# Cross-attention keys made in the opening of the self-attention in front, norm and queries batch by batch in its loop, masks by quarters

## The reference

```python
# both, per head: softmax(q @ k.T * 8**-0.5 + mask) @ v, then a projection
L0_attn  (sublayer 0):  q, k, v from norm(x); no mask
L0_xattn (sublayer 1):  q from norm(x); k, v from ctx; mask: valid keys of each batch (a row per batch)
L3_attn  (sublayer 9):  q, k, v by a down projection to 32 and up again; full 256 x 256 mask
L3_xattn (sublayer 10): q from norm(x); k, v from ctx; full 256 x 512 mask
```

## Time and profile before

| | us |
|---|---|
| median of 3 runs | 1529.12 (1528.99 to 1529.28) |
| the profiled execution | 1515.46 |
| its span, first to last instruction | 1513.4 |
| mean granted TensorE clock | 0.882 |
| PE / DVE / ACT / POOL busy | 1214.5 / 915.8 / 695.4 / 252.3 |

### The profile page before, as it was taken

How to read it: one execution, slowest core, us unless ns; L and a number is a source line. 1 busy time by engine, 2 the same in 40 slices (tenths; PEclk the granted TensorE clock), 3 DMA queues, 4 the chain that set the end, 5 groups by cost and what they waited for, 6 DMA issues and landing times. The chain is left out here.

```text
span 1513.4 us, 25902 instructions
## 1 busy us (share of the span) xinstructions
PE 1214.5 (80%) x9175; PEld 746.5 (49%) x9217; DVE 915.8 (61%) x2378; ACT 695.4 (46%) x1316; POOL 252.3 (17%) x525
## 2 busy tenths in 40 slices
PE   3877997686596398567999999999949669869993
PEld 1333434584243398355666666666638524323332
DVE  5658874334576454775676766666641365487746
ACT  2654883132442022213666665656605225436653
POOL 1211210453010255100000000000017312121110
PEclk8797999898798599677999999999968869979995
DMA  5525111584702466100000000000047451051100
GB/s 148 128 84 142 54 30 79 187 280 133 155 2 91 145 233 214 27 1 0 1 1 1 1 2 1 1 1 1 1 127 230 124 136 24 2 139 44 41 3 14
DMA packets 85600, 114.55 MB, mean 76 GB/s; under 512 B 11281, under 2 KB 65758, under 8 KB 85198
## 3 DMA queue, kind: packets, MB, share of 16 engines
q1 hardware_dynamic: 81026, 103.78, 23.2%
q0 software_dynamic: 4448, 9.12, 2.1%
HBM read 85.79 MB, written 26.61 MB: 74 GB/s over the span
## 5 line engine op out<-in xcount | busy, mean ns | idle before, releaser
L664 DVE TENSOR_REDUCE mx<-ps 128x4 f32<-128x1024 f32 (+1 forms) x128 | 153.4, 1221 | 53.2 <-PE ps L601 44.8
L2240 DVE CUSTOM_DVE_ANT_0 wring<-ps,probs 128x768 f32<-128x768 f32 x128 | 122.5, 957 | 57.0 <-PE ps L2112 56.8
L807 PE MATMUL ps<-probs,vaug 128*32 128x256 f32 (+1 forms) x1792 | 143.4, 394 | 13.4 <-ACT probs L775 9.2
L2196 ACT COPY qs<-ps 128x768 f32<-128x768 f32 x128 | 102.3, 800 | 97.7 <-PE ps L2119 97.7
L765 ACT ACTIVATE probs<-ps 128x1024 f32<-128x1024 f32 x96 | 98.2, 1023 | 86.5 <-PE ps L639 86.5
L770 ACT ACTIVATE probs<-ps 128x512 f32<-128x512 f32 x192 | 106.2, 594 | 38.7 <-PE ps L727 36.7
L236 POOL TENSOR_TENSOR rstd<-veps,mhalf 128x8 f32<-128x8 f32 x14 | 23.2, 1657 | 595.2 <-DVE veps L221 564.9
L2178 ACT ACTIVATE wring<-wring,r 128x768 f32<-128x768 f32 x128 | 120.8, 944 | 2.9 <-DVE r L2243 2.9
L2119 PE MATMUL ps<-ident,wring 128*128 128x128 f32 x768 | 110.4, 281 | 3.2 <-DVE wring L2277 3.2
L601 PE MATMUL ps<-ks,qs 49*128 49x256 bf16 (+1 forms) x512 | 84.0, 369 | 27.2 <-DVE mx L659 10.6
L2119 PEld LDWEIGHTS ps<-ident,wring 128*128 128x128 f32 x768 | 84.6, 141 | 39.4 <-issue 35.3
(11 more groups left out here) (311 smaller groups left out, 2334.2 us busy)
## 6 DMA issues: line engine op xcount, KB each, us to landing
wring<-in_L_ffn_w SPq DMA_DIRECT2D x19, 768.0 KB, 5.8
wring<-in_L_ffn_w SPq DMA_DIRECT2D x32, 384.0 KB, 4.6
wring<-in_L_ffn_w SPq DMA_DIRECT2D x19, 514.0 KB, 4.9
scr_q<-probs SPq DMA_DIRECT2D x10, 384.0 KB, 3.5
scr_k<-probs SPq DMA_DIRECT2D x27, 128.0 KB, 4.1
qs<-scr_q SPq DMA_DIRECT2D x18, 192.0 KB
probs<-in_L_ffn_w SPq DMA_DIRECT2D x8, 384.0 KB, 4.5
probs<-in_L_ffn_w SPq DMA_DIRECT2D x4, 768.0 KB, 6.3
```

The lines of the kernel that those rows point to most:

```text
L664: dve.tensor_reduce(out, src, AX.X, ALU.max, negate=True).then_inc(a_max.sem, 1)
L807: ins = pe.matmul(ps[32 * j:32 * j + 32, self.av_bank(s), q0:S], vaug[:, s % 2, kt, j, :], probs[:, s % 2, j, at:at + S - q0], start=(kt = ...
L2196: act.copy(self.pT[:, g % 2, j, :, k * P:(k + 1) * P], self.buffer("turn", i, 0, KV).rearrange("p (t n) -> p t n", n=P)).then_inc(self.out ...
L2240: dve.tensor_tensor_reduce(self.sc[:, s, :], src, self.maskb[:, u // (2 * PR), :], 1.0, -3.0e38, ALU.add, ALU.max, self.top[:, s:s + 1]).t ...
```

## The change

Two pairs are linked, L0_attn to L0_xattn and L3_attn to L3_xattn (`next`, `prev`).

- Keys of the cross-attention: all four projections in the opening of the self-attention, behind its values (`keys_tensor`); ScalarE evicts and casts part one (`keys_scalar`). In the first groups of its loop GpSimd subtracts (`key_r_gpsimd`), ScalarE casts part two behind the turned maxima (`key_p2_scalar`), GpSimd writes part three (`key_p3_gpsimd`). `ahead_sync` spills them between groups 4 and 9.
- Norm and queries: as a batch of the self-attention is summed, its statistics, power, `h`, transposes and query projection run in the loop of the next batch (`ahead_at`, `ahead_masked_at` say at which step; `beside` for TensorE, `evicted` for ScalarE). Batch 3 has only its statistics there; the rest is in the loop of the cross-attention, which also makes the values.
- SyncE loads keys and queries of batch 0 in groups 11 and 15; for that it waits at group 10 until the self-attention has read the part of `ks` that they overwrite. Mask rows of L0_xattn are written per batch, and cast on GpSimd in the opening. `ctxT`, the early weights and `mask_row` are loaded at the very start, so `late_inputs` has bundles for eleven groups, not thirteen.
- `x_done` is kept between the two; norm, projections and the idle matmuls of the cross-attention are gone.
- A mask pair is four matmuls of 64x64 (`mask_tensor`): row half `r` of the array makes bank `at + r`, in two column halves; the crosswise halves come from copies of the masks with their partition halves swapped (`m3a_half`, `m3x_half`, four DMAs before sublayer 9).

The core of the diff:

```diff
+        def keys_tensor(self, pe):
+            if self.n == 1:
+                pe.wait_ge(written, 16 * 4)
+            pe.wait_ge(proj_f.sem, proj_f.at(self.n - 1, 4))
+            for i in range(B):
+                pe.matmul(bank(i), wt(f"{self.name}_k"), ctxT[:, i * S2:(i + 1) * S2], start=True, stop=True).then_inc(proj_mm.sem, 1)
...
+        def keys_scalar(self, act):
...
+                act.activation(self.key_full(i), bank(i), ACT.Identity, bias=bcol[:, col:col + 1]).then_inc(proj_f.sem, 1)
...
+                act.copy(self.key_part(i, 0), self.key_full(i)).then_inc(proj_p1.sem, 1)
+        def key_r_gpsimd(self, pool, i):
...
+            pool.tensor_tensor(self.key_full(i), self.key_full(i), self.key_part(i, 0), ALU.subtract).then_inc(proj_r.sem, 1)
...
+        def stats_vector(self, dve, b):
+            dve.wait_ge(y_out.sem, y_out.at(self.n - 1, b + 1))
+            for j in (2 * b, 2 * b + 1):
+                ins = dve.bn_stats(stats[:, j, :], x[:, j, :])
...
+        def hT_tensor(self, pe, b):
+            pe.wait_ge(ln_h.sem, ln_h.at(self.norm, b + 1))
...
+            for t in range(2):
+                ins = pe.transpose(bank(6, S + t * P, S + t * P + P), h[:, 2 * b + t, :], ident[:, :])
...
+        def q_scalar(self, act, b):
...
+            act.activation(self.q_full(b), bank(6, S, 2 * S), ACT.Identity, bias=bscaled[:, col:col + 1], scale=SCALE).then_inc(proj_f.sem, 1)
+            act.wait_ge(proj_f.sem, proj_f.at(n, 4 + b + 1))
+            act.copy(self.q_part(b, 0), self.q_full(b)).then_inc(proj_p1.sem, 1)
...
+        def ahead_sync(self, sp, g):
+            n = self.n
+            if 4 <= g < 10:
+                for j in (2 * g - 8, 2 * g - 7):
+                    self.key_spill_sync(sp, j % 4, j // 4)
+            if g == 10:
+                sp.wait_ge(b_mm.sem, b_mm.at(n - 1, 2 * NQ * units[n - 1]))
+                if self.mask == "row":
+                    self.mask_sync(sp, 0)
+            if g == 11:
+                self.key_load_sync(sp, 0, 0, 8)
+            if 12 <= g < 15:
+                self.q_spill_sync(sp, 0, g - 12)
+            if g == 15:
+                self.q_load_sync(sp, 0, 0, 8)
+        def late_sync(self, sp):
+            for b in (1, 2):
+                for k in range(3):
+                    self.q_spill_sync(sp, b, k)
+            sp.wait_ge(b_mm.sem, b_mm.at(self.n - 1, G * units[self.n - 1]))
+        def ahead_at(self, s, u):
+            if self.next:
+                steps = {(9, 2): "n_stats", (10, 0): "n_h", (12, 0): "qr", (12, 2): "qp2", (13, 0): "qp3"}
+                for b in range(B):
+                    what = steps.get((s - 4 * b, u))
+                    if what and (b < 3 or what == "n_stats"):
+                        yield what, b, 0
+            elif self.prev:
+                steps = {(0, 2): [("val", 0), ("val", 1)], (0, 3): [("n_h", 3)], (0, 4): [("v_sb", 1)], (0, 6): [("v_sb", 0), ("val", 2), ("val", 3)],
+                         (1, 0): [("v_sb", 2)], (1, 2): [("v_sb", 3)], (6, 2): [("qr", 3)],
+                         (6, 5): [("qp2", 3)], (7, 2): [("qp3", 3)]}
...
+        def ahead_masked_at(self, t):
+            if self.next:
+                steps = {17: "n_stats", 18: "n_h", 23: "qr", 24: "qp2", 25: "qp3"}
...
+        def beside(self, o):
+            if self.next and 6 <= o and o % 4 >= 2:
+                yield ("n_tp", "nq")[o % 4 - 2], o // 4 - 1, o
...
+        def mask_tensor(self, pe, at, mask, swapped):
+            for r, lo in ((0, 0), (1, 1), (0, 1), (1, 0)):
+                rows, out = slice(HALF * r, HALF * r + HALF), slice(HALF * lo, HALF * lo + HALF)
+                pe.matmul(ps[out, at + r, :], identb[rows, rows], (mask if lo == r else swapped)[rows, :],
+                          start=True, stop=False, skip_group_check=True)
...
-                mask = m3x[:, 1, kt0 * S:(kt0 + 2) * S] if self.cross else m3a[:, 1, :]
-                for r in range(2):
-                    pe.matmul(bank(2 + b % 2 * 2 + r), identb[:, :], mask, start=True, stop=False, skip_group_check=True)
+                at = slice(kt0 * S, (kt0 + 2) * S)
+                if self.cross:
+                    self.mask_tensor(pe, 2 + b % 2 * 2, m3x[:, 1, at], m3x_half[:, at])
+                else:
+                    self.mask_tensor(pe, 2 + b % 2 * 2, m3a[:, 1, :], m3a_half[:, 1, :])
...
-                for r in range(0 if self.cross else 2):
-                    pe.matmul(bank(self.a_bank(a) + r), identb[:, :], m3a[:, 0, :], start=True, stop=False, skip_group_check=True)
+                if not self.cross:
+                    self.mask_tensor(pe, self.a_bank(a), m3a[:, 0, :], m3a_half[:, 0, :])
...
-                for _ in range(0 if s == 4 else 8 if ahead else 15):
+                for _ in range(0 if s == 4 or s in subs and subs[s].prev else 15):
                     pe.matmul(bank(5), identb[:, :], m3a[:, 0, :], start=True, stop=True)
```

More of the change, by code:

```diff
@@ L279, in __init__ @@
             self.v_bank = [6, 7, 4, 5]
-            self.chunk_order = [2, 3, 0, 1, 4, 5] if self.cross else [0, 2, 1, 3]
+            self.chunk_order = [0, 2, 1, 3]
+            self.next = self.prev = None
         def qv(self, g, c, r, rows, lo=0, hi=S):
@@ new lines, in late_sync @@
+        def late_sync(self, sp):
[14 more added lines that the diff above has]
+                         (6, 5): [("qp2", 3)], (7, 2): [("qp3", 3)]}
+                for what, b in steps.get((s, u), ()):
+                    yield what, b, 0
@@ L307, in chunk_tensor @@
             query, c = self.chunk(i)
-            if query or not self.cross:
-                pe.wait_ge(ln_hT.sem, ln_hT.at(self.norm, c + 1))
+            pe.wait_ge(ln_hT.sem, ln_hT.at(self.norm, c + 1))
             cols = slice(c * 512, c * 512 + 512)
@@ L342, in project_tensor @@
                 ins.then_inc(v_mm.sem, 1)
+            if self.next:
+                self.next.keys_tensor(pe)
         def project_vector(self, dve):
@@ L589, in a_tensor @@
                 pe.wait_ge(rows_in.sem, rows_in.at(n // 3, 4))
-            if k == 0 and self.mask == "row":
-                pe.wait_ge(mask_in.sem, mask_in.at(0, 2 * B))
             if k >= 2:
@@ L908, in order_masked @@
                     yield "masked", t, 0
+                if v % n == 0 and 0 <= o < G:
+                    yield from self.beside(o)
                 if self.cross:
@@ L973, in order_plain @@
                         yield "turn", s - 1, 0
+                    yield from self.ahead_at(s, u)
                 if s < G:
@@ L976, in order_plain @@
                 if 0 <= o < G:
+                    yield from self.evicted(o)
                     yield "o", o, 0
@@ L1033, in gpsimd @@
                     self.split_gpsimd(pool, s)
+                    if self.next and s < B:
+                        self.next.key_r_gpsimd(pool, s)
+                    if self.next and 1 <= s <= B:
+                        self.next.key_p3_gpsimd(pool, s - 1)
+                    if self.prev and s == 1:
+                        bias_gpsimd(pool, self.sub, self.norm, f"{self.name}_o")
+                if what == "n_stats":
+                    self.next.rstd_gpsimd(pool, s)
     MOES = [dict(name="L0_ffn", sub=2, experts=32, chunks=2, shared=1, choices=1, gate_at=0),
@@ L2479, in program @@
     attn = [Attention(0, 0), Attention(1, 1), Attention(2, 3), Attention(3, 12), Attention(4, 13)]
+    for first, then in ((0, 1), (3, 4)):
+        attn[first].next, attn[then].prev = attn[then], attn[first]
     subs = {t.sub: t for t in attn}
@@ L2627, in _ @@
                 others[s].tensor(pe)
-CONSTS = 1
+CONSTS = 2
 N_SUB_RUN = N_SUB
```

398 lines of the change are left out of this document (270 added, 128 removed).

## The result

| | before | after |
|---|---|---|
| timed runs side by side, median of 20 each | 1529.05 us (1520.90 to 1535.14) | 1520.58 us (1511.32 to 1529.68) |
| ratio, 95% interval | | 0.9948 (0.9930 to 0.9965) |
| the profiled execution, span | 1515.46, 1513.4 us | 1519.38, 1517.2 us |
| mean granted TensorE clock | 0.882 | 0.877 |

The change gains 0.5%, 8.5 us, where the forecast said 31 us and a range that ended at 1513. The profiled execution of before is also faster than any of its twenty timed runs (1520.90 at the least), so the two whole spans can't be set against each other.

A forecast was written before the change was run, and what follows sets the result against it. It took the seams to be bound by a chain of engines waiting for each other, the loops mostly by TensorE. Terms summed to -31.2 us: profiled 1515.46 becomes 1484.3, plus 13.7 for timed runs, 1498 us; range 1484 to 1513.

The forecast's parts named there:

- Seams (-32.7): Between self- and cross-attention: last output sum to first exponents shortens by 16.2 us in L0 and 16.5 in L3.
- Masks by quarters (-13): L3 stages: four 64x64 matmuls run side by side, saving 0.22 us per mask; 9.0 us in L3_attn, 4.0 in L3_xattn.
- Rivals 1 and 3: Mask quarters: overlap only in pairs, total 1511 us, chance 0.18; or run in a line, total 1543 us, chance 0.06.
- rival 4: Clock: lighter masks thin TensorE out and L3_attn stays at the lower level; total 1513 us, chance 0.03.
- Work moved into the loops (+6 in L0_attn): L0_attn's loop: TensorE's 1.0 us and 0.8 of waiting per batch, 5.4, plus 0.6 for casts.
- Rival 2: Loops: ScalarE's passes hold back exponents, SyncE holds back maxima; 12 us more, 1510, at full bound 1522; chance 0.15.
- Its named sign: L0_attn, first scores to last sum: some 85 us expected; over 92 would mean that the loops are dear.
- The same in L3_attn (+4): L3_attn's loop: inserted work costs 4.0 us, as VectorE idles about 1.0 per step and masks give TensorE room.
- SyncE (+1.5, and "covered" in the cross-attention): L0_attn: 3.65 us of added issuing less about 2 of slack; L0_xattn: 5.9 with mask rows, called covered.
- Batch 3 (+2): Cross-attention loops: batch 3's inserted part costs 1.0 us of TensorE in each, 2.0 in all.
- openings (+1.0): Self-attention openings: four key projections ahead of the first scores cost 1.0 us, bounds 0 to 2.

The follow-up runs named there:

- constants: The changed kernel with four order moves, and VectorE's conversion of masks and constants moved from the first seam into L0_xattn's tail; ratio to before 0.9807.
- quarters alone: The kernel before with only the masks by quarters and the four copies that make the swapped halves; ratio to before 0.9948.
- whole: The changed kernel with the masks of both L3 stages as whole arrays again; ratio to before 0.9978.
- later: The changed kernel with the transposes of batches 0 and 1 issued one group later in both fused loops; ratio to before 0.9914.
- the combination: The changed kernel with transposes one group later, query copy behind osb, batch 0's keys loaded in the tail, mask rows ahead; ratio to before 0.9831.
- three: The changed kernel with mask rows ahead, batch 0's keys loaded in the tail and query copy behind osb, without later transposes; ratio to before 0.9839.
- together: Another name for the combination: the changed kernel with all four order moves; ratio to before 0.9831.

## Why the prediction was wrong, step by step

**Seams (-32.7): right in mechanism, -30.1.** First exponents 17.0 us behind the sum, not 16, and 15.9, not 14. The masks and constants on VectorE, priced at 2.1 us, took 2.1 (123.90 to 126.00), and "constants" shows that 2.0 of it can be had by doing them elsewhere. The working has two small slips: its terms give 11.45 us and not 11.6 in the first seam, and 1334.6 and not 1335.0 in the second.

**Masks by quarters (-13): right in mechanism, too large, about -8.** Four tiles do run at once: mask to scores 0.33 us, as foretold. The steady step fell from 2.33 to 2.09 us, also as foretold. But 6.6 us came out in L3_attn, not 9.0, and 1.7 in L3_xattn's last three batches (0.3 in the whole stage), where I had 4.0. In L3_attn the 23 steps from the ninth maximum to the last gave 5.2 us (57.7 before, 52.5 with quarters alone), the 5.3 that I had for them. Missing are two smaller terms. From the first scores to the ninth maximum 0.9 came out, where I had 2.7: only four of the early steps before were 2.90 to 3.04 us long, not eight, and with quarters one more step, of 3.04, lay at the lower clock. Behind the last maximum 0.5 came out, where I had 1.0. Rivals 1 and 3 are refuted, and rival 4 too for L3_attn, whose clock was 1.00 from 1265 to 1325 us.

**Work moved into the loops (+6 in L0_attn): this step failed.** I priced TensorE's own time (1.0 us a batch) and 0.8 for ScalarE's passes ahead of `osb`, 5.4 in three batches; from the first sum to the last it took 18.6 more. The 0.96 for the latter is there. What I left out is the wait for `h` itself: I had listed norm on VectorE at 0.55 as work beside TensorE's, and never asked where TensorE's transposes stand in relation to it. They stand one maximum of 1.23 us too early, and TensorE waits 1.77. With 0.37 more ahead of the projection that is 1.0 + 1.77 + 0.96 + 0.37 = 4.1 us a batch, against 3.9 measured in the first step of the kernel with whole masks (18.4 against 14.5), whose clock stayed up. In the same places the clock may fall, and the step is 20.5. And the tail (9.2 before, 16.3 after) has batch 2's chain in it: in the kernel with whole masks TensorE waits 1.65 for `h`, 0.77 and 1.31 for `osb`, at half the clock. I had given that batch the same price as the others, though nothing lies beside it there. Rival 2, with 12 us more and "at the full bound 1522", is what happened in size; I gave it 0.15. Of its two causes, ScalarE's passes and SyncE's late maxima, both are there (0.96 and 2.03 us at a place), but the longest wait in L0_attn, for `h` behind a maximum on VectorE, is in neither. Its named sign, over 92 us in L0_attn, came out at 93.9, though the same L0_attn took 90.3 in "whole".

**The same in L3_attn (+4): +6 or more.** The loop has 88.5 us with quarters alone and 94.4 to 98.3 with the inserts.

**SyncE (+1.5, and "covered" in the cross-attention): wrong in both places.** In L0_attn the six key loads cost little by their issuing. They delay the landing of the rows behind them, for which TensorE waits 3.29 us in "later", 1.03 to 2.24 in three others and not at all in the changed kernel, where it is late already. In L0_xattn I compared 5.9 us of issuing with a group of 5.7 and called it covered. At the place shown it was 1.40 + 3.61 + 0.80 + 1.55 = 7.4, since the six key loads took 3.61 to issue and not 2.3, and the stage lost 3.1 us to it.

**Batch 3 (+2) and openings (+1.0): a little more each,** +2.5 for the openings; the part of L0_xattn that the mask rows don't explain is 2.3 us, and L3_xattn gives back what its quarters gain.

So 24 us are missing: 8 in L0_attn (11, had its first batch not gained 3), 4.4 in L0_xattn, 4.3 in L3_attn, 2.8 in L3_xattn, 2.6 in the seams and 1.5 in the openings. Most of the first two is order, not work: the combination has it back with the same instructions, at 85.9 us in L0_attn, which is 7.6 more than before where I had +7.5. That agreement is partly luck. Its first batch is 2.2 us shorter than before, which I had not forecast. From the first sum to the last it is 9.8 longer: 1.9 and 1.2 in the two steps of the body, within the 1.8 a batch that I had priced, and 6.7 in the tail. What stays open is how the rest of "three" and "together" compare, and why the same stall sometimes brings the clock down and sometimes doesn't.

## What to carry to other kernels

When work is put into a loop whose engine is full, price not the work but the wait at each place where the full engine meets it: find the producer's place in its own queue, and add what stands ahead of it there. A wait that is removed can uncover the next one, so try moves in pairs before you call one useless. A loop's tail has little beside it to cover a chain: here the same insert cost 1.2 to 1.9 us in the body and 6.7 in the tail, once the order in the body was right.

## What the runs showed of the hardware

- The same idle stretch of 1.77 us of TensorE, at the same point of the same loop, was followed by the lower clock in one execution and not in another. Two kernels with the same L0_attn, from 65 to 75 us, columns as in the earlier trace rows, the last but two the clock; first the one with mask rows ahead:

```profile
65.00:70.00 5.00, 3.23 (x33) 1.27 (x31) 3.50 (x10) 2.33 (x6) 1.85 (x6) 0.85 0.62 196
70.00:75.00 5.00, 4.99 (x34) 2.14 (x30) 2.86 (x5) 2.70 (x7) 1.04 (x5) 0.50 0.32 107
```

  Then the one with whole masks:

```profile
65.00:70.00 5.00, 3.23 (x44) 1.59 (x39) 3.40 (x10) 2.48 (x6) 1.84 (x6) 1.00 0.54 181
70.00:75.00 5.00, 4.37 (x44) 1.81 (x40) 3.68 (x7) 3.67 (x11) 1.44 (x7) 1.00 0.32 106
```

  The first step from batch to batch was 20.5 us in the first and 18.4 in the second.
- Four 64x64 tiles with 512 columns each take 0.24 us in all, on two banks and two row halves, and the change of tiling costs about 0.09 us on either side: 0.37 from the transposes where it was 0.28 without a change, and 0.33 to the scores.
- Two small DMAs (3 KB each), issued by 84.25 us and 4 us after the first of six loads of 768 KB together, held TensorE until 88.89; the DMA engines' busy share was 0.83 and 0.88 in the two stretches from 80 to 90 us. At 195.85, behind six loads of 192 KB together and with the share at 0.19 to 0.29, it took 2.7 us from the start of issue to TensorE's start.
- Issuing six loads took SyncE between 2.25 and 3.74 us in the loop of L0_xattn of the changed kernel, for the same sizes.
